# Graph attention on one core: two small subtractions per strip go from VectorE to GpSimd

## What is computed

```python
for i in range(L):                      # L = 4
    Q = _ln(h @ Wq[i], gq[i], bq[i]);  K = _ln(h @ Wk[i], gk[i], bk[i])
    qi = Q[src];  kj = K[dst]
    score = (qi * kj).sum(-1) + 0.1 * (edge_attr * qi[:, :RBF]).sum(-1) + logm[dst]
    smax = jax.ops.segment_max(score, src, num_segments=N)
    es = jnp.exp(jnp.minimum(score - smax[src], 20.0))
    denom = jax.ops.segment_sum(es, src, num_segments=N)
    aggi = jax.ops.segment_sum((es / (denom[src] + 1e-10))[:, None] * (h[dst] @ Wm[i]), src, num_segments=N)
```

## Time and profile before

| what | us |
|---|---|
| median of three executions | 14316.78 |
| lowest, highest | 14309.37, 14319.74 |
| the profiled execution | 14305.02 |
| its span, first to last instruction | 14303.3 |
| PE busy in the span | 11578.7 (81%) |
| DVE busy | 12194.2 (85%) |
| ACT busy | 8167.6 (57%) |
| POOL busy | 7231.4 (51%) |

### The profile page before, as it was taken

The page is one execution under the profiler, slowest core; times in us unless marked ns, Lnnn a source line. Parts: engine busy times, 40 slices in busy tenths (PEclk is TensorE's granted clock), DMA queues, the critical chain, the costliest instruction groups (busy, mean ns, idle before and its releaser), DMA issues.

```text
span 14303.3 us, 630454 instructions
## 1 busy us (share of the span) xinstructions
PE 11578.7 (81%) x196113; PEld 9877.2 (69%) x196113; DVE 12194.2 (85%) x29979; ACT 8167.6 (57%) x26006; POOL 7231.4 (51%) x9217
## 2 busy tenths in 40 slices
PE   2899999986765888988987988988997767686566
PEld 2666666775665877777776877777776666576556
DVE  5788888767898899988998899988998889699997
ACT  0344444345676688867886788867885302067630
POOL 0566666634453654535553655545552355565436
PEclk9999999999855955576555955586555678685586
DMA  9322222464797877757774877757775976589957
GB/s 381 99 60 60 60 60 60 52 101 156 273 286 210 308 189 190 190 186 248 190 190 124 311 189 190 187 208 231 193 193 174 304 204 218 146 293 282 248 190 204
DMA packets 3472139, 2731.34 MB, mean 191 GB/s; under 512 B 2332483, under 2 KB 3076116, under 8 KB 3471750
## 3 DMA queue, kind: packets, MB, share of 16 engines
q1 hardware_dynamic: 2746678, 1045.93, 29.0%
q0 software_dynamic: 236192, 860.68, 20.7%
q10 hardware_dynamic: 489008, 821.78, 15.4%
HBM read 1616.59 MB, written 1110.81 MB: 191 GB/s over the span
## 4 chain that ended last, share of the span: by engine, by line
PE 26%; DVE 25%; DMA 14%; issue 14%; ACT 10%; DVEq 5%; SPq 4%; ACTq 1%; POOL 1%; POOLq 0%
DMA chunk_layer_rows<-arena 7%; DVE arena L1886 6%; PE ps L1160 5%; PE ps L1151 5%; ACT arena L1021 4%; DVE arena L1813 3%; DMA arena<-edge_hot_b 3%; PE ps L1307 3%; PE ps L1342 2%; DVEq L109 2%; PE ps L1274 2%; PE ps L1143 2%; ACT arena L847 2%; PE ps L1180 2%; DVE arena L1791 2%
## 5 line engine op out<-in xcount | busy, mean ns | idle before, releaser
L1307 PE MATMUL ps<-arena 128*128 128x49 bf16 x56160 | 2596.5, 213 | 879.7 <-DVE arena L1829 421.0
L1307 PEld LDWEIGHTS ps<-arena 128*128 128x128 fp8e4 x56160 | 2336.1, 115 | 1193.8 <-issue 1182.8
L1274 PE MATMUL ps<-block_tables,arena 128*128 128x98 bf16 (+2 forms) x56160 | 2449.2, 201 | 603.0 <-DVE arena L1799 305.9
L1274 PEld LDWEIGHTS ps<-block_tables,arena 128*128 128x128 bf16 (+1 forms) x56160 | 2220.6, 99 | 831.9 <-issue 394.6
L743 POOL COPY block_tables<-arena 128x294 bf16 (+2 forms) x2340 | 1445.1, 618 | 2211.1 <-PE ps L1274 1293.2
L957 ACT ACTIVATE arena<-ps 128x392 f32<-128x392 f32 (+1 forms) x3900 | 1711.5, 480 | 1053.1 <-PE ps L1274 640.7
L705 POOL DMA_INDIRECT edge_records<-arena x1563 | 1558.9, 997 | 1227.3 <-DVE arena L1585 834.5
L727 POOL DMA_INDIRECT arena<-chunk_layer_rows,map_a x1040 | 1043.2, 1003 | 2018.8 <-ACT arena L1021 1929.7
L1021 ACT ACTIVATE arena<-arena,small 128x49 f32<-128x49 f32 x8320 | 1996.8, 323 | 102.1 <-ACT small L1013 0.7
L1799 DVE TENSOR_SCALAR arena<-arena,iota_row 128x1024 bf16<-128x1024 uint8 x2080 | 1567.4, 754 | 113.7 <-PE ps L1274 60.7
L1886 DVE CUSTOM_DVE_ANT_0 arena<-ps,arena 128x1024 bf16<-128x1024 f32 x1040 | 1273.4, 1224 | 321.4 <-PE ps L1342 211.0
(11 more groups left out here) (323 smaller groups left out, 20530.3 us busy)
## 6 DMA issues: line engine op xcount, KB each, us to landing
chunk_layer_rows<-arena ACTq DMA_DIRECT2D x1040, 392.0 KB, 3.3
arena<-node_hot_a SPq DMA_DIRECT2D x1820, 128.0 KB
arena<-edge_hot_a SPq DMA_DIRECT2D x1560, 128.0 KB
chunk_gated<-arena ACTq DMA_DIRECT2D x520, 324.0 KB, 2.7
arena<-edge_records SPq DMA_DIRECT2D x1040, 160.0 KB
chunk_rows<-arena ACTq DMA_DIRECT2D x780, 196.0 KB, 2.0
arena<-edge_records SPq DMA_DIRECT2D x520, 196.0 KB
arena<-edge_hot_b SPq DMA_DIRECT2D x780, 128.0 KB
```

The lines of the kernel that those rows point to most:

```text
L1274: last = pe.matmul(psv[:, 2 * r + j // tpb, (j % tpb) * w:(j % tpb + 1) * w], hot[:, s, j * P:(j + 1) * P], bt4[:, s, i, 0:w], start=i == ...
L1307: last = pe.matmul(to[s % 2], he4j[:, s % 4, j, :], low_part(i, s, j), start=j == 0 and i == 0, stop=j == C8 - 1 and i == 2)
```

## The change

`middles` and `low` leave VectorE's list. GpSimd makes them in a new function `lower_parts`, which `collect` calls as `ahead(k)` before each gather in the four attention stages: for k it makes the middle parts of strip k-6 and the low part of the maximum of strip k-7. So gather(k) now stands behind "red" of strip k-6 and "max" of strip k-7 besides "ph" of strip k-8. After the last gather three more turns are run, for the last strips' parts.

```diff
-            def gather(tab, w, map_, used, base, after=None):
+            def gather(tab, w, map_, used, base, after=None, ahead=None):
 
                 for k in range(NS):
+                    if ahead is not None:
+                        ahead(k)
                     if k >= 8:
                         pool.wait_ge(used, base + k - 7)
...
-                gather(tab, w_row, map_a, used, base, after)
-                for k in range(NS, NS + 4):
+                gather(tab, w_row, map_a, used, base, after, ahead)
+                for k in range(NS, NS + (4 if ahead is None else 7)):
+                    if ahead is not None:
+                        ahead(k)
                     after(k)
...
+            def lower_parts(l, k):
+                if 0 <= k < NS:
+                    pool.wait_ge(at["red"], l * NS + k + 1)
+                    pool.tensor_tensor(sc4[:, k % 4, C8:2 * C8], sc4[:, k % 4, 0:C8], sch4[:, k % 4, 0:C8, 1], ALU.subtract).then_inc(at["mid"], 1)
+                if 1 <= k < NS + 1:
+                    r = (k - 1) % 2
+                    pool.wait_ge(at["max"], l * NS + k)
+                    pool.tensor_tensor(mx3[:, r, 1:2], mx3[:, r, 0:1], mxh[:, r, 0, 1:2], ALU.subtract).then_inc(at["low"], 1)
...
-                collect(ed_l, ROWL, at["ph"], l * NS, WK, at["q"], l * NS, lambda k: keys(l, k))
+                collect(ed_l, ROWL, at["ph"], l * NS, WK, at["q"], l * NS, lambda k: keys(l, k), lambda k: lower_parts(l, k - 6))
...
-                def middles(k, s):
-                    dve.wait_ge(at["red"], base + k + 1)
-                    dve.tensor_tensor(sc4[:, s % 4, C8:2 * C8], sc4[:, s % 4, 0:C8], sch4[:, s % 4, 0:C8, 1], ALU.subtract).then_inc(at["mid"], 1)
...
-                def low(k, s):
-                    r = s % 2
-                    dve.wait_ge(at["max"], base + k + 1)
-                    dve.tensor_tensor(mx3[:, r, 1:2], mx3[:, r, 0:1], mxh[:, r, 0, 1:2], ALU.subtract).then_inc(at["low"], 1)
...
-                walk(nc, dve, NS, [(2, shifted), (0, products), (1, READ), (1, peak), (0, reduced), (1, raised, True), (0, middles), (1, low),
+                walk(nc, dve, NS, [(2, shifted), (0, products), (1, READ), (1, peak), (0, reduced), (1, raised, True),
```

More of the change, by code:

```diff
@@ L755, in source_block, with collect @@
                 pool.tensor_copy(st4[:, k % 4, :, 0:w], of[:, :, 0:w]).then_inc(st_made, 1)
-            def collect(tab, w_row, used, base, w, picked, picked_base, more=None):
+            def collect(tab, w_row, used, base, w, picked, picked_base, more=None, ahead=None):
                 def after(k):
```

## The result

| | us |
|---|---|
| kernel before, median (4 runs beside it) | 14313.08 |
| changed kernel, median of 4 | 14438.47 |
| ratio, 95% interval | 1.0092, 1.0074 to 1.0109 |
| forecast | 14577, that is +260; measured +125 |

What follows compares the result with a forecast made beforehand. The loop through middles, transpose and peak was taken to bound the attention stages: period 4.34 to 4.59 us, +0.25 x 1040 = +260 us, 14317 + 260 = 14577; range 14,250 to 14,880, likeliest case 14,530 to 14,770.

Steps and rivals of the forecast that it cites:

- What bounds it, and that the loop rises: Attention stages: the loop peak, red, mid, transpose, pick_max, spread_s, peak sets the pace and goes from 4.15 to 4.55 us.
- The block: Middles on GpSimd, starting inside once, is held back 0.31 us; the transpose starts 0.40 us later.
- The rule of the Trainium skill that the prediction cites: A VectorE instruction with both inputs in SBUF contends with GpSimd's SBUF read; issue order decides which blocks.
- The release 115 ns after the end: Skill figure for GpSimd's release after VectorE: middles would end at about +0.82, the loop be near 4.82 us.
- The ratio of about two for elementwise work: Skill figure: GpSimd about half as fast as VectorE, an estimate of 0.33 us for middles.
- Low: Low on GpSimd slips in before twice, ends at +0.65, hidden behind the transpose by 0.1 us.
- Everything behind the transpose keeps its distance: Attention loop: pick_max +0.86, spread_s +1.41 to +2.44, peak +2.84; loop 4.15 + 0.40 = 4.55 us.
- the turn of 4.15: Tight turn in the earlier trace, peak to next peak, taken as the loop's length: 1.71 + 2.44 us.
- The allowance of 0.04: Mean strip period above the tight turn, kept from 0.19 us before; makes the period 4.59 us.
- The lower end of 14,530: Lower bound in us of the likeliest case; middles' work of 0.09 us gives a period of 4.56.
- The gather's new place at nothing: Gather, copy and keys on GpSimd start later but finish with 1.6 us to spare, so no cost.

Runs made afterwards that it cites:

- experiment 6: The changed kernel with two useless small subtractions put on VectorE behind twice: 14439.58 us, against 14438.47 without them.
- experiment 1: The changed kernel with low back on VectorE between raised and once, only middles on GpSimd: 14235.56 us, ratio 0.9946 to the kernel before.
- experiment 5: The changed kernel with one added wait on VectorE, once also waiting for middles of the same turn: 14332.59 us, ratio 1.0016 to the kernel before.
- experiment 11: The kernel before with two spare small one-operand reduces added on VectorE, on a chip where the kernel before takes 15301.73 us: ratio 0.9998.
- experiment 4: The kernel before, both subtractions on VectorE, with only the changed kernel's waits on GpSimd ahead of each gather: 14238.23 us, ratio 0.995.
- e9: The kernel before with each gather also waiting until twice of the strip eight behind is done: 14245.84 us, ratio 0.995.
- e10: Only middles on GpSimd, each gather also waiting until twice of the strip eight behind is done: 14276.12 us, ratio 0.9973 to the kernel before.
- e12: Only low on GpSimd, with once made to wait for low of its turn: ratio 1.0425 to the kernel before.
- experiment 7: The kernel before with two useless small subtractions added on VectorE behind twice: 14512.93 us, ratio 1.0138.
- experiment 8: The kernel before with the block-number read and add_raised moved ahead of once on VectorE: 15216.86 us, ratio 1.0631.

## Why the prediction was off

**What bounds it, and that the loop rises: right.** The chain peak, red, mid, transpose, pick_max, spread_s, peak closes 1034 of 1040 turns of the changed kernel, and VectorE's relief bought nothing (experiment 6).

**The block: right in kind and size.** Middles was to end at +0.55 and the transpose to start at +0.66. They came at +0.60 and +0.65: the work is 0.20 and not the 0.12 that I took; a start at +0.08 instead of +0.12 and an answer within 0.05 us instead of 0.11 made up for it, which is luck. (The wait in the earlier trace rows from which I had the start was for L1421 on VectorE's queue, not for the cast.) Unheld it would have ended at +0.28 (experiments 1 and 5); 0.32 us of 0.52 is the block. The release came 0.14 before once's end (5505.96 less 0.20 of work, against 5505.90), as the earlier trace rows had it. The rule of the Trainium skill that the prediction cites ("SBUF — State Buffer", section "Who interferes with whom") agrees with these rows: the one that came second was held. The release 115 ns after the end, of the section "A bandwidth-pool intuition that's wrong" there, is not what the rows show for this pair; the page measured it on DMA descriptors behind a copy. The ratio of about two for elementwise work ("GPSIMD Engine Reference", section 3) isn't seen at this size: 0.20 on GpSimd, 0.17 on VectorE.

**Low: right.** It ran from +0.56 to +0.75, ahead of pick_max at +0.90. The edge was thin: twice started 0.02 behind it.

**The step that failed: "Everything behind the transpose keeps its distance".** From the transpose to the peak I took 2.18 us from the tight turn of before (+0.26 to +2.44), as if all of it belonged to the loop. It is 2.09 now (+0.65 to +2.74). In the earlier trace rows spread_s ended at 5516.82 and the peak started 0.40 later, with no wait for PE noted on its row, and products had ended 0.14 before it; in the changed kernel it starts 0.31 after spread_s, and its row names PE. The kernel before showed the same 0.31 one turn earlier, where the peak at 5513.07 does name PE:

```profile
5511.73 1.03 PE L1342 MATMUL ps<-scores_turned,select_row 16*128 16x128 bf16 x8 [0.21 <-ACT scores_turned L999]
```

So the rows say that the turn of 4.15 had been closed 0.09 late by something other than the loop, VectorE's order by its place behind products, and I had added 0.40 to a number that held both. The 0.09 are 94 us of the forecast; with the transpose at +0.65 instead of +0.66 the loop is 4.45 instead of 4.55, 104 us. What the changed kernel's distance is, 2.09, is measured. That VectorE's order was what closed the turn before is read from rows alone: experiment 11, which should have cost 20 to 100 us in that case, cost nothing measurable.

**The allowance of 0.04: too large.** The mean of the four stretches, 4.455, is 0.005 above the loop; the rest of VectorE's and ACT's work had slack in nearly every turn. 35 us. The two terms together are 139 us, and 260 - 139 = 121 against 125 measured. They close by construction, since both are read from the changed kernel's own loop and mean. (The lower end of 14,530 was also 16 us below what its 4.56 gives.)

**The gather's new place at nothing: wrong for the kernel before, without effect on the sum.** In the kernel before it is worth 71 us (experiment 4). In the changed one the loop may cover it; no run has the changed kernel with the gather in its old place. Seen so, the change is a gain of 71 us by the waits and a loss of 200 by giving the subtractions to GpSimd behind once (experiment 4 against the changed kernel).

**What stays open:** what gains the 71 us, since shorter subtractions (e9) and VectorE's load (e11) are no full answer; what sets the mean of 4.34 in the kernel before, whose peak waits for PE in only 448 of 1040 turns; and why e10 and e12 are slow.

The best versions found are e1, which keeps low on VectorE and moves middles alone, at 14235.56, 0.54% under the kernel before and 1.4% under the changed one, and e4, which moves only the gather, at 14238.23. They can't be told apart, so no run shows a gain from moving work off VectorE.

## What to carry to other kernels

Before a small step moves from VectorE to GpSimd, look at what VectorE issues next: if that has two operands in SBUF and GpSimd's step lies on a chain, the step can take nearly as long as that neighbour (here 0.52 us beside 0.56). A wait or a short instruction between the two can be worth more than the work that was moved (106 us in experiment 5, against nothing measurable for the work). And when a chain is lengthened, measure its links in a turn in which that chain was late, never in one that another order had closed.

## What the runs showed of the hardware

The block between the two engines works both ways. A GpSimd subtraction of 128x8 takes 0.20 us, or 0.52 when it starts 0.10 behind once, and it goes on 0.14 before once's recorded end. A VectorE subtraction of 128x8 took 1.05 instead of 0.15 (experiment 7), and one of 128x392 took 1.39 instead of 0.57 (experiment 8), when they started inside the table copy and keys came right behind it: VectorE did not get in between the two. A reduce with one operand in the same place was never longer than 0.155 (1040 times, experiment 11). The gather on GpSimd's queue is held as well: 982 ns in the median in the kernel before, 1212 in experiment 1, where it starts inside once. A busy share said nothing about the bound here: with 636 of 700 us busy, VectorE took two more unheld instructions of 0.15 us a strip without a measurable change in the time (experiment 11).
